# All sixteen tiles through the shared network ahead of the experts, and gated expert rows added to the output in memory

## The chip, the cores and the metric

The kernel is one program on one core of one Trainium2 chip. Its time is the device time of one execution in microseconds (us). The kernel before was timed three times: 1279.81, 1280.91 and 1282.57 us, median 1280.91 us.

## The reference

The layer takes x, 32 batches of 64 rows of 512 floats (2048 tokens), and a context of 1601 rows for each batch. It is three residual blocks, each on the layer norm of its input:

```
x = x + xattn(layernorm(x), ctx)      # similarity to the context, softmax, four features @ W_qv
x = x + attn(layernorm(x))            # 16 heads of 32, causal, 64 rows a batch
x = x + ffn(layernorm(x))
# ffn, h = layernorm(x) of 2048 tokens:
probs = softmax(h @ w_router.T)                     # 8 experts
weight, expert = top_k(probs, 2); weight /= sum(weight)
inter = square(relu(h_of_expert @ w1[e].T))         # 512 -> 512
y     = inter @ w2[e].T                             # 512 -> 512
moe   = sum over both choices of weight * y
shared = square(relu(h @ ws1.T)) @ ws2.T            # 512 -> 1024 -> 512
out   = shared + moe
```

The change is in the third block alone. Every token gets three terms added to its row of x: the shared network, and two gated expert rows.

## The kernel before

The tokens are 16 tiles of 128 rows (T = 16), held in X in on-chip memory. Stage a (the context attention) runs to about 555 us, stage b (the 16-head attention) to about 838 us, and the third block takes the rest. All engines run programs written out by hand: each has its own order of instructions, and they meet at semaphores only. There is no planner. SP issues nearly all DMAs, in one queue; POOL issues the indirect ones.

The third block has these parts.

- **Router.** VectorE (DVE) normalises each tile, TensorE (PE) transposes it (the transposed tiles are h2T), the router's logits are taken, and DVE works out the two experts of each token, their weights (`wt0`, `wt1`, L1672 and L1673) and the slot of each choice (`slot_i`). Slots are rows of `moe_in`, in groups of 128 rows with one expert each: GT = 39 groups, since each expert's last group is padded. `scattered_norm` makes the normed rows of a tile and POOL sends them out with two indirect DMAs (L753), 32 in all.
- **Shared network ahead of the experts.** Tiles 0 to 11 (TA = 12) go in six pairs. PE's `shared(p)` (L2306) does the first layer of pair p in four groups (`shared_group`, at L2064) and then the second layer of both tiles of pair p-1 (`shared_second`, at L2054). Each product is made in three passes, of a high and a low part of every operand, both of type fp32r. ScalarE (ACT) takes the relu and the high part, DVE squares and takes the low part (`shared_rest`), and `residual_c` adds the result to X, counted by `x3_ready`. The transposed tiles 12 to 15 (`h2T_late`) are stored to `h2T_away` by SP (L538), since they stand where the weights of expert 1 go.
- **Weights.** SP loads the high parts of all experts' weights with `load_w1` (L528) and `load_w2` (L532). The last of them, `load_w1(0, 1)` (L601), waits until the first layer of the last pair is done (`sh_done`), since its place holds that pair's data; PE waits for it at L2386, before the first expert group.
- **Experts.** For each group g, SP loads the low parts of the weights where the expert changes (L573) and the 128 rows of the group (L595, four DMAs). DVE transposes the rows (L1642); PE makes the first layer of g and the second layer of g-1 (L2345, L2348, L2351); DVE copies the result from PSUM to one of two buffers `yg` (L1781, counted by `y_ready`); SP stores it to `moe_out` (L625). PE needs the copy of group g-1 before it writes its bank again (L2375).
- **End.** Tiles 12 to 15 go through the shared network after the experts, in float32 and one pass: PE at L2404 and L2412, 32 products each, with weights loaded again. At the same time POOL gathers the two expert rows of each of 16 tiles by indirect DMA (L764), DVE multiplies by the weights and adds them to X (`mix`, L1806 and L1807), and SP stores each tile (L645). X of tiles 0 to 7 was stored to `x_away` and is loaded back.

## Time and profile before

| | us |
|---|---|
| timed runs | 1279.81, 1280.91, 1282.57 |
| the profiled execution's own time | 1278.48 |
| its span, first to last instruction | 1276.8 |
| PE busy | 1251.5 (98%), 7654 matmuls |
| DVE busy | 763.6 (60%) |
| ACT busy | 364.6 (29%) |
| POOL busy | 173.8 (14%) |
| TensorE clock granted, mean | 0.999 |

The span runs from the first to the last instruction of any engine; 1.7 us of the execution lie around it. "Busy" is time in which an engine had an instruction under way. The matmuls' ends are modelled, so a busy PE is not PE at its peak. A DMA's "landing" is the time from its issue to its completion.

### The profile page before, as it was taken

How to read it: one execution, taken by the hardware profiler on the slowest of the kernel's cores; microseconds unless marked ns; L12 is line 12 of the kernel's file. 1: busy time of each engine (PE TensorE's matmuls, PEld its weight loads, DVE VectorE, ACT ScalarE, POOL GpSimd, SP SyncE). 2: the span in 40 equal slices, each digit the busy share in tenths (PEclk: the TensorE clock that was granted, in tenths of full speed). 3: DMA queues.
4: the chain of work that ended last, by engine and by line, in shares of the span. 5: the costliest groups of instructions: out<-in, count | busy, mean ns of one | idle time of the engine just before them, and what ended most of it. 6: DMA issues, size and time to landing. Idle time of an engine off the chain costs nothing.

```text
span 1276.8 us, 21920 instructions
## 1 busy us (share of the span) xinstructions
PE 1251.5 (98%) x7654; PEld 844.2 (66%) x7655; DVE 763.6 (60%) x1409; ACT 364.6 (29%) x593; POOL 173.8 (14%) x159
## 2 busy tenths in 40 slices
PE   5999999999999999999999999999999999999998
PEld 3344444444444444467888888899998888888843
DVE  4456555655454444478988877857543555555556
ACT  2322211212121211244555454542222233332300
POOL 1000000000000000003222223601430000000055
PEclk9999999999999999999999999999999999999999
DMA  9999999999999999833788778731749545554587
GB/s 353 411 418 416 415 415 419 419 419 418 419 419 416 392 396 390 316 134 123 253 285 276 256 266 305 281 132 59 275 170 333 169 155 188 186 185 158 170 324 247
DMA packets 103763, 375.95 MB, mean 294 GB/s; under 512 B 10656, under 2 KB 33184, under 8 KB 88992
## 3 DMA queue, kind: packets, MB, share of 16 engines
q1 hardware_dynamic: 98592, 358.52, 73.6%
q0 software_dynamic: 5120, 16.78, 3.7%
q8 instruction: 28, 0.46, 0.1%
q14 instruction: 23, 0.19, 0.0%
HBM read 368.45 MB, written 69.73 MB: 343 GB/s over the span
## 4 chain that ended last, share of the span: by engine, by line
PE 86%; DMA 7%; DVE 3%; issue 1%; ACT 1%; SPq 1%; POOL 0%; ACTq 0%; DVEq 0%; POOLq 0%
PE ps L1992 14%; PE ps L1880 13%; PE ps L2064 9%; PE ps L2054 9%; PE ps L2345 6%; PE ps L2348 6%; PE ps L2351 6%; DMA parts_low<-split 5%; PE ps L1955 4%; PE ps L1838 3%; PE ps L2412 2%; PE ps L2404 2%; PE ps L1970 2%; DMA arena<-ctx_n 2%; PE ps L1930 1%
## 5 line engine op out<-in xcount | busy, mean ns | idle before, releaser
L1992 PE MATMUL ps<-arena 128*64 128x512 f32 (+1 forms) x832 | 193.1, 596 | 0.0
L1880 PE MATMUL ps<-arena 128*64 128x512 f32 (+1 forms) x1024 | 177.6, 503 | 1.9 <-DVE arena L1138 1.2
L2064 PE MATMUL ps<-split 128*128 128x256 f32 x1344 | 170.6, 285 | 2.6 <-DVE split L1337 2.3
L2064 PEld LDWEIGHTS ps<-split 128*128 128x128 f32 x1344 | 163.7, 191 | 7.2 <-issue 4.7
L1880 PEld LDWEIGHTS ps<-arena 128*64 128x64 f32 x1024 | 65.0, 137 | 122.0 <-issue 119.4
L1992 PEld LDWEIGHTS ps<-arena 128*64 128x64 f32 (+1 forms) x832 | 58.4, 137 | 113.2 <-issue 112.6
L1234 DVE SCALAR_TENSOR_TENSOR arena<-arena,hbar 128x512 f32<-128x512 f32 x128 | 90.5, 749 | 67.9 <-PE ps L1955 66.3
L772 ACT ACTIVATE arena<-ps 128x512 f32<-128x512 f32 (+1 forms) x93 | 52.2, 581 | 241.9 <-PE ps L1955 180.2
L2054 PE MATMUL ps<-split 128*128 128x512 f32 x384 | 96.6, 400 | 1.1 <-DVE arena L1405 1.1
L1208 DVE TENSOR_TENSOR F<-arena,ps 128x512 f32<-128x512 f32 x16 | 11.0, 688 | 135.9 <-ACT split L817 135.9
L678 POOL TENSOR_TENSOR arena<-arena,row_b 128x512 f32 (+1 forms) x16 | 20.2, 1268 | 475.5 <-DVE arena L1108 448.1
L2054 PEld LDWEIGHTS ps<-split 128*128 128x128 f32 x384 | 69.7, 188 | 17.6 <-issue 2.0
L764 POOL DMA_INDIRECT arena<-moe_out,slot_i x32 | 34.0, 1063 | 271.4 <-DMA moe_out<-arena 262.0
L1955 PE MATMUL ps<-arena 128*64 128x512 f32 x256 | 66.0, 594 | 0.3 <-DVE arena L1234 0.3
L2054 PE MATMUL ps<-split_ws,split 128*128 128x512 f32 x264 | 61.1, 390 | 0.0
L817 ACT ACTIVATE split<-ps 128x256 fp32r<-128x256 f32 x32 | 10.5, 381 | 163.9 <-PE ps L1860 163.9
L2054 PEld LDWEIGHTS ps<-split_ws,split 128*128 128x128 f32 x264 | 49.2, 188 | 10.0
L772 ACT ACTIVATE arena<-arena 32x512 f32<-32x512 f32 x64 | 40.3, 630 | 34.0 <-DVE arena L1352 30.8
L1055 ACT ACTIVATE row_a<-ps 128x512 f32<-128x512 f32 x39 | 23.3, 598 | 82.1 <-PE ps L2351 82.1
L2345 PE MATMUL ps<-w_high,xT_p 128*128 x156 | 45.8, 415 | 0.2 <-issue 0.2
L753 POOL DMA_INDIRECT moe_in<-arena,idx x32 | 33.1, 1035 | 89.1 <-DVE idx L1736 81.7
L1838 PE MATMUL ps<-ident,arena 128*128 128x128 f32 x256 | 37.2, 276 | 8.0 <-DVE arena L1108 6.7
(229 smaller groups left out, 2007.5 us busy)
## 6 DMA issues: line engine op xcount, KB each, us to landing
arena<-ctx_t SPq DMA_DIRECT2D x122, 800.5 KB, 17.0
high<-parts_low SPq DMA_DIRECT2D x78, 1024.0 KB
arena<-ctx_n SPq DMA_DIRECT2D x96, 768.0 KB, 13.5
arena<-ctx_n SPq DMA_DIRECT2D x32, 1024.0 KB, 14.8
parts_high<-split SPq DMA_DIRECT2D x16, 1024.0 KB, 8.7
parts_low<-split SPq DMA_DIRECT2D x16, 1024.0 KB, 10.5
moe_in<-zero SPq DMA_DIRECT2D x3, 3328.0 KB, 17.5
moe_out<-arena SPq DMA_DIRECT2D x39, 256.0 KB, 2.1
```

Of the source, the lines that this page charges most:

```text
L764: nc.gpsimd.indirect_dma_start(y01[k][i], None, moe_out, bass.IndirectOffsetOnAxis(ap=slot_i[k][:, t:t + 1], axis=0)).then_inc(y01_in[i % ...
L772: return nc.scalar.activation(o, i, ACT.Copy)
L1234: v.scalar_tensor_tensor(Wc[:, h, :], w_qv_sb[:, 3 * KD + k, :], hbar[:, i, k, h:h + 1], w_qv_sb[:, k, :], ALU.mult, ALU.add).then_inc(wc_ ...
L1838: last = nc.tensor.transpose(dst[:, P * k:P * (k + 1)], src[:, P * k:P * (k + 1)], ident[:, :])
L1880: last = mm(bank(n)[S * h:S * (h + 1), 0:w], qT[:, k, S * h:S * (h + 1)], ctxT[h][:, k, at_j:at_j + w], start=(k == 0), stop=(k == KD - 1))
L1955: last = mm(bank(5)[r, :], F1[i][:, k, r], Wc[:, h, :], start=False, stop=(k == KD - 1))
L1992: last = mm(bank(7)[S * h:S * (h + 1), :], ET[0:w, c, S * h:S * (h + 1)], ctxN[h][0:w, c, :], start=(c == 0), stop=(c == JC - 1))
L2054: last = mm(dst, lhs[a][:, k, :], rhs[b][:, k, :], start=(k + i == 0), stop=(k == n - 1 and i == 2))
L2064: last = mm(dst[:, 2 * P * m:2 * P * (m + 1)], w[a][:, k, c], tokens[b][:, k, :], start=(k + i == 0), stop=(k == KD - 1 and i == 2))
L2345: mm(dst, parts[0][:, k, :], high_w(k), start=(k == 0), stop=False)
L2348: mm(dst, parts[1][:, k, :], high_w(k), start=False, stop=False)
L2351: last = mm(dst, parts[0][:, k, :], low_w(k), start=False, stop=(k == KD - 1))
```

## The change

- `TA` becomes T: all 16 tiles go through the shared network ahead of the experts, in eight pairs. ACT's and DVE's programs have pairs 5 and 6 written out after their loops, without a scatter; PE's loop runs two rounds more. The float32 shared network after the experts goes, with `h2T_away`, the second loads of ws1 and ws2, `x_away` and `moe_out`.
- `out` has 128 rows more than the result, for padded slots; the host drops them. SP stores X with the shared network's part straight to `out` (`store_rows`, five DMAs in all with one that zeroes the extra rows).
- A new table `slot_info` in device memory holds for each of the 39 x 128 slots the token's row and its weight, 8 bytes a slot. SP fills it for empty slots (row 2048 + partition, weight 0); POOL writes the entries of the tokens with 32 indirect DMAs, two a tile; SP waits for all of them and loads the table into `of_slot` with one DMA, ahead of `load_w1(0, 1)` in its queue. DVE turns the rows into integers (`token_i`).
- DVE's copy of each group's result becomes a product by the slot's weight, from `of_slot`.
- POOL adds each group's 128 rows to `out` by one indirect DMA with accumulate; it waits for the DMA of the group before, since two groups may hold the same token. The gathers, `mix`, and the stores at the end go.
- `load_w1(1, 2)` moves behind the low weights of group 0 and waits for the low part of tile 15; `load_low2(g + 1)` waits for PE's `y_done` in place of `y_ready`.

```diff
 TY = (TX + T) // 2
-TA = 3 * T // 4
+TA = T
 TH = T // 2
-TL = T - TR
 S16 = B * S // P
...
     moe_in = nc.dram_tensor("moe_in", [GT * P, D], F32).ap()
-    moe_out = nc.dram_tensor("moe_out", [GT * P, D], F32).ap()
-    x_away = nc.dram_tensor("x_away", [T * P, D], F32).ap()
-    h2T_away = nc.dram_tensor("h2T_away", [P, KD, (T - TR) * P], F32).ap()
+    slot_info = nc.dram_tensor("slot_info", [GT * P, 2], F32).ap()
     parts_high, parts_low = ([nc.dram_tensor(f"{n}{i}", [E * P, KD * D], F32).ap() for i in range(2)]
                              for n in ("parts_high", "parts_low"))

...
+        no_token = sb("no_token", [P, 2])
         cdot, smax, nsmax, smx, erow, rs = (small[:, i:i + 1] for i in range(6))
         bmax, nbmax, bsum, brec = (per_batch[:, i, :] for i in range(4))

         slot_i = [sb(f"slot_i{k}", [P, T], I32) for k in range(2)]
         eg_i = sb("eg_i", [P, GT], I32)
...
             for q in range(1, ZEROED):
                 zero_slots(q)
+            sp.wait_ge(pool_filled, NOTOKEN)
+            info_v = slot_info.rearrange("(g p) c -> p g c", p=P)
+            sp.dma_start(info_v, no_token[:, :].unsqueeze(1).to_broadcast([P, GT, 2])).then_inc(info_filled, 16)
...

             load_w1(5, E)
-            for t in range(TR, T):
-                sp.wait_ge(r_h2T_ready, t + 1)
-                sp.dma_start(h2T_away[:, :, P * (t - TR):P * (t - TR + 1)], h2T_late[t - TR]).then_inc(h2T_moved, 16)
-            sp.wait_ge(h2T_moved, 16 * TL)
-            sp.wait_ge(lg_done, T)
-            load_w1(1, 2)
-
-            away = x_away.rearrange("(t p) d -> p t d", p=P)
+
...
             read_group(0)
             load_low1(0)
-            sp.wait_ge(x3_out, 32)
+            sp.wait_ge(x3_out, 48)
             load_w2(ARENA + KD * D, 7, 8)
+            sp.wait_ge(lg_done, T)
+            sp.wait_ge(h2lo_ready, T)
+            load_w1(1, 2)
+            sp.wait_ge(x3_ready, TR)
+            store_rows(slice(TH, TR))
             for i in range(2):
                 sp.wait_ge(scat[i], 32 * (T // 2))

...

             load_slots(0)
+            sp.wait_ge(info_out, 16 * 2 * T)
+            sp.dma_start(of_slot[:, :, :], info_v).then_inc(info_in, 16)
...
+            sp.wait_ge(x3_ready, T)
+            store_rows(slice(TR, T))

...
                     sp.wait_ge(xgT_ready, g + 2)
                     load_slots(g + 3)
-                if g > 0:
-                    sp.wait_ge(y_ready, g)
-                    sp.dma_start(moe_out[P * (g - 1):P * g, :], yg[(g - 1) % 2]).then_inc(y_out[(g - 1) % 2], 16)
                 if g + 1 < GT:
+                    if g > 0:
+                        sp.wait_ge(y_done, g)
                     load_low2(g + 1)
-                if g in LATE_WS1:
-                    k = LATE_WS1.index(g)
-                    sp.wait_ge(y_done, S16 * (k // 2 + 1))
-                    sp.dma_start(ws1_l[:, k:k + 1, :], ws1t.rearrange("(k p) n -> p k n", p=P)[:, k:k + 1, :]
-                                 ).then_inc(ws_in, 16)
-                if g == GT - 2:
-                    sp.wait_ge(in_done, GT)
-                    sp.dma_start(h2T_l, h2T_away).then_inc(h2T_moved, 16)
-            sp.wait_ge(y_ready, GT)
-            sp.dma_start(moe_out[P * (GT - 1):P * GT, :], yg[(GT - 1) % 2]).then_inc(y_out[(GT - 1) % 2], 16)
-            sp.dma_start(X[:, 0:TH, :], away[:, 0:TH, :]).then_inc(x3_back, 16)
-            sp.dma_start(ws2_l, ws2t.rearrange("(k p) n -> p k n", p=P)).then_inc(ws_in, 16)
-
-            def store_out(t):
-                sp.wait_ge(mix_ready, MIX.index(t) + 1)
-                if t >= TR:
-                    sp.wait_ge(x3_ready, t + 1)
-                sp.dma_start(out_v[:, t:t + 1, :], X[:, t:t + 1, :]).then_inc(out_sem, 16)
-
-            for t in (*range(TH, TR), 0, 1, 2, TR, 3, 4, TR + 1, 5, 6, 7, TR + 2, TR + 3):
-                store_out(t)
-            sp.wait_ge(out_sem, 16 * T)
+            sp.wait_ge(x3_out, 16 * 5)


         @block.gpsimd
...
                         ).then_inc(scat[i], 16)

-            pool.wait_ge(y_out[0], 16 * (GT // 2 + 1))
-            pool.wait_ge(y_out[1], 16 * (GT // 2))
-            for i, t in enumerate(MIX):
-                if i >= 4:
-                    pool.wait_ge(y01_in[i % 4], 32 * (i // 4))
-                    pool.sem_inc(hold, 1)
+            pool.wait_ge(info_ready, 2)
+            pool.wait_ge(pool_filled, IOTA)
+            pool.wait_ge(info_filled, 16)
+            for t in range(T):
                 for k in range(2):
                     nc.gpsimd.indirect_dma_start(
-                        y01[k][i], None, moe_out, bass.IndirectOffsetOnAxis(ap=slot_i[k][:, t:t + 1], axis=0)
-                    ).then_inc(y01_in[i % 4], 16)
+                        slot_info, bass.IndirectOffsetOnAxis(ap=slot_i[k][:, t:t + 1], axis=0), info[k][:, t, :], None
+                    ).then_inc(info_out, 16)
+
+            pool.wait_ge(token_ready, 1)
+            pool.wait_ge(x3_out, 16 * 5)
+            for g in range(GT):
+                pool.wait_ge(y_ready, g + 1)
+                if g > 0:
+                    pool.wait_ge(y_out[(g - 1) % 2], 16 * ((g - 1) // 2 + 1))
+                nc.gpsimd.indirect_dma_start(
+                    out, bass.IndirectOffsetOnAxis(ap=token_i[:, g:g + 1], axis=0), yg[g % 2], None,
+                    compute_op=ALU.add).then_inc(y_out[g % 2], 16)
+            pool.wait_ge(y_out[(GT - 1) % 2], 16 * ((GT - 1) // 2 + 1))
+            pool.wait_ge(y_out[GT % 2], 16 * (GT // 2))


...
             dve.wait_ge(lg_read, 2)

-            def shared(p, scatter):
+            def shared(p, scatter=None):

                 shared_start(p)
-                scattered_norm(scatter)
+                if scatter is not None:
+                    scattered_norm(scatter)
                 shared_residuals(p)
-                scattered_norm(scatter + 1)
+                if scatter is not None:
+                    scattered_norm(scatter + 1)
                 shared_rest(p)

...
             step(v.tensor_tensor(vs, v0, v1, ALU.add))
             step(v.reciprocal(vs, vs))
-            step(v.tensor_tensor(wt0[:, :], v0, vs, ALU.mult))
-            step(v.tensor_tensor(wt1[:, :], v1, vs, ALU.mult))
+            v.tensor_tensor(info[0][:, :, 1], v0, vs, ALU.mult).then_inc(info_ready, 1)
+            v.tensor_tensor(info[1][:, :, 1], v1, vs, ALU.mult).then_inc(info_ready, 1)
...
                 shared(p, scatter=2 * p - 2)
             shared(4, scatter=6)
+            for p in range(5, TA // 2 - 1):
+                shared(p)
...
                     if not (isinstance(stores, int) and stores == 0):
                         dve.wait_ge(y_out[i], 16 * stores)
-                    v.tensor_copy(yg[i], bank(3)).then_inc(y_ready, 1)
+                    gate = of_slot[:, bass.ds(g - 1, 1), 1:2].rearrange("p o c -> p (o c)")
+                    v.tensor_scalar(yg[i], bank(3), gate, None, ALU.mult).then_inc(y_ready, 1)
...
             for i in range(2):
                 residual_c(TA - 2 + i, i)
+            dve.wait_ge(info_in, 16)
+            v.tensor_copy(token_i[:, :], of_slot[:, :, 0]).then_inc(token_ready, 1)
             for g in range(1, 4):
...
             experts(GT - 1, True, True, False, out=out_of(GT - 1))
             experts(GT, False, True, False, out=out_of(GT))
-
-
-            def mix(i):
-                t = MIX[i]
...
-                dve.wait_ge(mix_ready, MIX.index(TR + u) + 1)
-                v.tensor_tensor(x_tile(TR + u), x_tile(TR + u), last_bank[u], ALU.add).then_inc(x3_ready, 1)
-
-            last_square(0)
-            last_square(1)
-            for m, i, n in ((2, 0, 2), (3, 2, 1), (4, 3, 1), (5, 4, 2), (6, 6, 1), (7, 7, 1)):
...
             experts(GT - 1)
             experts(GT, now=False)
-            pe.wait_ge(ws_in, 32 + 16 * KD)
-            pe.wait_ge(h2T_moved, 16 * (TL + 1))
-            pe.wait_ge(x3_ready, TA)
-            for m in range(KF):
...
-            pe.wait_ge(ws_in, 48 + 16 * KD)
-            for u in range(TL):
-                for k in range(KF):
-                    if u == 0:
-                        pe.wait_ge(lsh_ready, k + 1)
-                    last = mm(last_bank[u], shT_l[:, k, P * u:P * (u + 1)], ws2_l[:, k, :],
-                              start=(k == 0), stop=(k == KF - 1))
-                last.then_inc(shared_done, 1)


...
     nc = bacc.Bacc("TRN2", target_bir_lowering=False, num_devices=1, dynamic_dma_scratch_size=4096)
     aps = [nc.dram_tensor(n, a.shape, mybir.dt.from_np(a.dtype), kind="ExternalInput").ap() for n, a in ins.items()]
-    out = nc.dram_tensor(_OUT, (B * S, D), F32, kind="ExternalOutput").ap()
```

## Rows read from the trace of the kernel before

**Rows 1.** The chain that ended last, its final pieces: start us, us, what.
```profile
1217.68 0.93 PE ps L2351 x4
1218.61 27.47 PE ps L2404 x64
1246.08 27.48 PE ps L2412 x64
1273.58 0.69 DVE arena L1818
```

**Rows 2.** Timeline of PE, last shared pairs and first expert group: start, us, instruction.
```profile
906.77 11.68 PE L2064 MATMUL ps<-split 128*128 128x256 f32 x96
918.28 11.07 PE L2054 MATMUL ps<-split_ws,split 128*128 128x512 f32 x48
929.19 11.68 PE L2064 MATMUL ps<-split 128*128 128x256 f32 x96
...
951.61 11.68 PE L2064 MATMUL ps<-split 128*128 128x256 f32 x96
963.12 11.07 PE L2054 MATMUL ps<-split_ws,split 128*128 128x512 f32 x48
974.43 1.20 PE L2345 MATMUL ps<-w_high,xT_p 128*128 x4 [0.23 <-issue]
```

**Rows 3.** Timeline of DVE: result copies of four expert groups, and a PSUM product.
```profile
1100.94 0.69 DVE L1781 COPY arena<-ps 128x512 f32<-128x512 f32 x1 [0.61 <-PE ps L2351]
1106.88 0.69 DVE L1781 COPY arena<-ps 128x512 f32<-128x512 f32 x1 [0.62 <-PE ps L2351]
1214.06 0.69 DVE L1781 COPY arena<-ps 128x512 f32<-128x512 f32 x1 [1.46 <-PE ps L2351]
1218.65 0.69 DVE L1781 COPY arena<-ps 128x512 f32<-128x512 f32 x1 [2.83 <-PE ps L2351]
1222.08 0.69 DVE L1812 TENSOR_SCALAR arena<-ps 128x512 f32<-128x512 f32 x1 [2.74 <-PE ps L2404]
```

**Rows 4.** Line L753 (the 32 indirect stores): its instructions, and issue to landing.
```profile
L753 POOL DMA_INDIRECT moe_in<-arena,idx x32: 958/974/1242, 888.1 to 958.8; - x32
DMA to landing us min/median/max: 2.7/3.0/8.3
```

**Rows 5.** Line L764 (the 32 gathers), the same two rows.
```profile
L764 POOL DMA_INDIRECT arena<-moe_out,slot_i x32: 942/1018/1333, 1221.9 to 1264.4; - x32
DMA to landing us min/median/max: 3.6/6.0/6.7
```

**Rows 6.** Stretches: engines' busy us, clock, DMA share, GB/s.
```profile
core 0: us, PE busy (x) PEld busy (x) DVE busy (x) ACT busy (x) POOL busy (x), PEclk, DMA share, GB/s
1050.00:1100.00 50.00, 50.00 (x238) 41.35 (x237) 28.53 (x43) 15.87 (x26) 0.00 (x0) 1.00 0.54 179
```

**Rows 7.** Timeline of SP's DMA issues before the first expert group.
```profile
965.95 1.75 SPq L595 DMA_DIRECT2D arena<-moe_in  x4
967.75 1.21 SPq L528 DMA_DIRECT2D w_high<-parts_high  x1
969.00 0.95 SPq L532 DMA_DIRECT2D high<-parts_high  x2
970.82 1.82 SPq L595 DMA_DIRECT2D arena<-moe_in  x4
972.68 0.45 SPq L532 DMA_DIRECT2D high<-parts_high  x1
```

**Rows 8.** DMAs issued in 967 to 974 us: count, KB each, median us to landing.
```profile
high<-parts_high SPq DMA_DIRECT2D x2, 2048.0 KB, 12.6
w_high<-parts_high SPq DMA_DIRECT2D x1, 1024.0 KB, 5.6
```

**Rows 9.** DMA in 1110.8 to 1114 us, a group's rows loaded: packets, queue's share.
```profile
DMA packets 577, 0.26 MB, mean 82 GB/s; under 512 B 65, under 2 KB 577, under 8 KB 577
q1 hardware_dynamic: 577, 0.26, 29.3%
```

**Rows 10.** Waits of SP's queue in 840 to 1000 us: total, times, longest.
```profile
SPq L593 <- DMA arena<-moe_in: 9.3, 1, 9.3
SPq L588 <- DMA moe_in<-arena,idx: 8.0, 1, 8.0
```

**Rows 11.** Timeline of SP's issues around the end of stage b.
```profile
802.32 8.51 SPq L500 DMA_DIRECT2D moe_in<-zero  x2
837.24 0.36 SPq L528 DMA_DIRECT2D w_high<-parts_high  x1
```

**Rows 12.** Timeline of PE: second layer of the first expert group.
```profile
988.54 1.17 PE L2345 MATMUL ps<-w_high,xT_p 128*128 x4
...
991.37 1.07 PE L2345 MATMUL ps<-high 128*128 x4
```

86 lines of the change are left out of this document (27 added, 59 removed).

## The prediction, made before the changed kernel ran

> **What bounds the kernel now.** I read the page's shares first, then the chain of waits, then the timelines of PE, DVE, SP and POOL around the changed places, and last the landings of the DMAs. The page gives PE as busy for 98% of the span, and the chain runs through PE to its end: the last second-layer product of the last expert group ends at 1218.61, two blocks of 64 float32 products follow, 27.47 and 27.48 us, and one DVE addition ends the arithmetic at 1274.3 of 1276.8 [rows 1]. So the time is a sum of PE's own durations. The pieces around the change are regular: one shared pair takes 22.42 us on PE, 906.77 to 929.19 to 951.61 [rows 2], and an expert group 5.94 us, 1100.94 to 1106.88 [rows 3]. No wait of note stands in either. The DMA engines are half used in the expert stage, a share of 0.54 [rows 6].
>
> **The part that goes.** Everything after 1218.61 goes: both float32 blocks, the gathers, the mixing, and the last stores. 1276.8 - 1218.61 = 58.2 us of the span. Gathers, mixing and the reload of X ran beside the float32 products and are worth nothing by themselves; with the products they go in full.
>
> **The part that comes instead, on PE.** Two more pairs, 2 x 22.42 = 44.8 us [rows 2]. The range of this term is small: in the pairs before, DVE also made and scattered two tiles' rows and PE still had no gap, and the new pairs have less on DVE. ACT and DVE run the same program a pair. DVE's, ACT's and PE's own durations in them I take as unchanged.
>
> **The new end.** After PE's last product DVE multiplies by the weight in place of a copy. A copy from PSUM took 0.69 us and so did a tensor-scalar product from PSUM [rows 3], so this edit is free in every group, and 0.04 + 0.69 us at the end. Then POOL issues the last accumulating DMA and waits for its landing. No row shows an accumulating DMA. The nearest is the plain indirect store of the same 128 rows of 2 KB, 3.0 us from issue to landing, 2.7 at the least and 8.3 at the most [rows 4]; the gathers, issued while the engines were full, took 3.6 to 6.7, median 6.0 [rows 5]. Below 2.7 it can't be, since it does all that the store does. I take 4.0: the store's 3.0 and one more for reading the old rows, at a time with no other transfer. With 0.3 for the last wait the end costs 0.7 + 4.0 + 0.3 = 5.0 us; by the bounds 3.7 to 9.3.
>
> **The accumulating DMAs before the last.** There are 39, each waits for the landing of the one before, and nothing else holds POOL, whose issue takes 1.0 us [rows 4]. They are hidden as long as one takes less than a group's 5.94 us from issue to landing. The cover is two `yg` buffers: DVE's product waits for the landing of two groups before, PE's next second layer waits for that product, so a landing that is late once is absorbed and a mean above 5.9 us is not. From 4.0 there are 1.9 us of room, and I cost this at nothing; by the upper row of the loaded gathers it costs (second rival). In bytes it takes the place of the store to `moe_out`, and adds a read of 256 KB a group; 179 GB/s on average at a share of 0.54 [rows 6] leaves room. The first one also waits for the last store of X, 1 MB queued behind the low weights of group 1; PE's chain waits for no accumulate until the third group's result, two groups later, so that is hidden.
>
> The Trainium skill (Collectives: The Full Stack, The bandwidth ceiling: the fold count and why AG ≠ RS ≠ AR) says that an add in the DMA path is slow by its second source read, with twice the read traffic, and not by the add. By that rule the transfer part of the 256 KB would double, an estimate of some 0.7 us, and the landing would be 3.7 in place of my 4.0, 0.3 us less in the sum.
>
> **The slot table.** POOL's 32 small indirect stores follow its last row store, 958.8 + 1.3, since the scatters stand in the same pairs as before [rows 4]. The gathers' starts are (1264.4 - 1221.9) / 31 = 1.37 us apart [rows 5]; 32 of them end at 960.1 + 43.9 = 1004, and with 3.0 us from the last issue all have landed at about 1006. SP is by then past `load_slots(0)` and its wait for the scatters, which in the kernel before still cost it 8.0 us [rows 10]. The last pair's first layer, 963.1 before, ends at 963.1 + 44.8 = 1007.9 [rows 2]. So the load of the table goes out at about 1006 and `load_w1(0, 1)` directly behind it at 1008.3, in the same queue. PE wants that weight at 974.19 + 44.84 = 1019.0 (974.43 less the 0.23 us of issue [rows 2]). Before, it was issued at 967.75 [rows 7] and landed 5.6 us later at 973.4 [rows 8], 0.8 us ahead of PE: this margin is thin, but SP now issues it 10.7 us ahead in place of 6.4.
>
> What eats this is the table's load itself. Slots of a group lie along the partitions, so the 39 x 128 entries of 8 bytes are 4992 separate pieces, 312 for each of 16 engines. The smallest pieces in the trace are the 512-byte ones of a group's rows: 577 packets in a share of 0.293 of 3.2 us and 16 engines, 26 ns each [rows 9]. By that the table takes 312 x 0.026 = 8.1 us, about 1007.5 to 1015.6; the weight's 1 MB needs some 3 us of the queue and its latency, and lands at 1019 to 1021. I take a stall of 1.0 us on PE. It can be 0 (smaller pieces may be quicker than 512 bytes) or, at four times 26 ns, (312 x 0.104 = 32.4 us, 24.3 more) about 25 us; nothing in the trace bounds it closer. The other weights behind it have more room: `load_w2(4, 6)`, issued at 972.68 and 12.6 us under way, was there by 985.3, and PE asks at 991.4 [rows 7, 8, 12].
>
> The Trainium skill (DMA: Bandwidth & Descriptors, Specifications) says that below 512 bytes a transfer is done as read-modify-write. That speaks against the table: if a piece then costs twice the 26 ns, the stall is 1.0 + 8.1 = 9.1 us, which is the first rival; no row has pieces this small.
>
> **Edits at nothing.** SP fills the table once with the same 4992 pieces after the zeroing of the slots, issued at 802, and its next load is only at 837.24 [rows 11]; that weight is used 150 us later. The stores of tiles 12 to 15 to `h2T_away` go; they lay beside PE. `load_w1(1, 2)` moves some 125 us later, to about 987, when the low part of tile 15 is done, still 32 us ahead of PE. `load_low2` waits for `y_done`, a copy earlier than before. Two weight products lose their step waits, four iotas and memsets come on POOL where it idles.
>
> **The sum**, against the profiled execution: 1276.8 - 58.2 + 44.8 + 5.0 + 1.0 = 1269.4 us of span, with 1.7 us around it 1271.1. The median of the timed runs stood 2.4 us above the profiled execution (1280.91 against 1278.48), so the forecast is 1273.5 us, 7.4 less than before. Its own range, from the bounds of the end and a stall of up to 3 us, is 1271 to 1280.
>
> **Rivals.**
> 1. *The table's load stands in front of the weight.* Every nanosecond over 26 a piece costs 0.31 us of PE. At 52 ns the time is 1281.6, at 58 the gain is gone, at 104 it is 1298. For: 8-byte pieces, the same queue, and the 0.8 us margin of before. Against: 512-byte pieces also carry their bytes, so a piece of 8 may be no slower. Chance 0.17, over 1278 to 1298.
> 2. *The accumulating DMAs become the chain* (the other side). The place is POOL's wait for the group before; it decides from 5.9 us on. At 6.7, the slowest gather, the 38 intervals cost 38 x (6.8 - 5.94) = 33 us and the time is 1306; at the slowest store, 8.3, 38 x 2.46 = 93 us and 1367. PE would then wait at L2375 in every group. For: one at a time, a read and a write in memory at both ends, full engines when an expert's weights load. Against: the median plain store at 3.0, and only some of the groups load weights. Chance 0.21.
> 3. *Something small eats it*: a landing of 8 us at the end (+4), or PE losing a little in each group to slower loads. 1276 to 1282. Chance 0.06.
>
> The forecast has 0.56. **Range and chances.** Two medians of this kernel can be told apart from 0.2%, 2.6 us on. The forecast's 0.56 is all faster but for 0.01. Rival 1 gives 0.02 faster, 0.05 same and 0.10 slower; rival 2 is slower, 0.21; rival 3 splits 0.03, 0.02, 0.01. Faster 0.60, same 0.08, slower 0.32. The range goes from 1270 to 1306, where the slower half of rival 2 is left out.
>
> **What would show it.** Right: PE without a gap from the first added pair to about 1263; no float32 block; a product at L1781's place every 5.94 us; the indirect DMAs landing in about 4 us; the end some 5 us after PE's last product. Rival 1 shows as one gap of PE ahead of the first expert group, with SP's weight landing late. Rival 2 shows as a gap of PE in each group, DVE waiting for an accumulating DMA, and a group's period equal to its landing. The forecast is wrong if either gap is over 5 us in sum, or a shared pair takes other than 22.4 us.

## The result, and the profile after

The changed kernel takes 1294.22 us in the median of four runs (1286.60 to 1298.28) against 1280.36 of the kernel before on the same chip: a ratio of 1.0107, with a 95% interval of 1.0083 to 1.0132. It is slower by 1.1%, where the forecast was 1273.5 us, 0.6% faster. The profiled execution is the quickest of the four, 1286.6 us with a span of 1284.9, so the trace explains 15.5 of the 20.7 us between forecast and median (1284.9 against the forecast span of 1269.4); the other executions have no trace. Here and below, a ratio is that of a kernel's time to the kernel before on the same chip, and the bracket behind it its 95% interval.

The page of the changed kernel: busy time by engine, then the groups of the chain, then POOL's accumulating DMA and the product by the weight.

```profile
PE 1244.3 (97%) x7814; PEld 861.6 (67%) x7815; DVE 743.3 (58%) x1382; ACT 376.1 (29%) x613; POOL 233.0 (18%) x202
...
DMA out<-arena,token_i 16%; PE ps L1950 14%; PE ps L2022 14%; PE ps L2012 13%; PE ps L1838 13%; PE ps L1913 4%; PE ps L1796 2%; PE ps L1928 2%; DMA arena<-ctx_n 2%; PE ps L1888 1%; PE ps L2041 1%; PE ps L1895 1%; PE ps L1892 1%; PE ps L1902 1%; PE ps L1900 1%
...
L742 POOL DMA_INDIRECT out<-arena,token_i x39 | 60.6, 1554 | 217.3 <-DMA out<-arena,token_i 151.4
...
L1768 DVE TENSOR_SCALAR arena<-ps,of_slot 128x512 f32<-128x512 f32 x39 | 29.3, 751 | 71.6 <-DMA out<-arena,token_i 60.2
```

PE is busy 7.2 us less than before and the span is 8.1 us longer. The chain, which before ran through PE to its last product [rows 1], now has 16% of accumulating DMAs in it. PE's timeline (start, us, instruction) shows how far the forecast holds:

```profile
904.00 11.68 PE L2022 MATMUL ps<-split 128*128 128x256 f32 x96
...
926.41 11.68 PE L2022 MATMUL ps<-split 128*128 128x256 f32 x96
...
948.84 11.68 PE L2022 MATMUL ps<-split 128*128 128x256 f32 x96
...
971.25 11.68 PE L2022 MATMUL ps<-split 128*128 128x256 f32 x96
...
1005.19 11.07 PE L2012 MATMUL ps<-split_ws,split 128*128 128x512 f32 x48
1016.09 1.07 PE L2303 MATMUL ps<-w_high,xT_p 128*128 x4
```

A pair is still 22.42 us, as in [rows 2], no gap stands ahead of the first expert group, and this execution came to that stretch 2.8 us earlier than the one before did. SP's queue shows why the first expert's weight was in time:

```profile
1005.27 0.38 SPq L583 DMA_DIRECT2D of_slot<-slot_info  x1
1005.70 2.66 SPq L512 DMA_DIRECT2D w_high<-parts_high  x1
```

```profile
of_slot<-slot_info SPq DMA_DIRECT2D x1, 39.0 KB, 4.7
```

The second fence is the list of DMAs (KB, us to landing): the table of 4992 pieces landed 4.7 us after its issue. What went wrong comes behind it, in POOL's adds (duration, first and last start, who is waited for, landings), where [rows 4] had 958 ns and 3.0 us:

```profile
L742 POOL DMA_INDIRECT out<-arena,token_i x39: 1550/1550/1611, 1037.8 to 1278.7; - x39
its engine sat idle before it (us, times) until:
  DMA out<-arena,token_i: 151.4, 32
  DVE arena L1768: 65.9, 7
who waited for it (us, times):
  POOL out L742: 151.4, 32
  DVE arena L1768: 60.2, 26
...
DMA to landing us min/median/max: 4.4/5.0/8.3
```

39 starts from 1037.8 to 1278.7 are 38 intervals of 6.34 us, against 5.94 for a group before [rows 3]. 32 of the 38 waited for the landing of the add before, and 26 times DVE then waited for its buffer. PE in turn waits for DVE's product (us in total, times, longest), which is a part of what it loses in the expert groups:

```profile
PE ps L2303 <- DVE arena L1768: 7.1, 4, 2.9
```

The last pieces of the chain (start, us, what) show two turns:

```profile
1268.01 4.40 DMA out<-arena,token_i
1272.40 0.02 issue
...
1272.45 0.71 issue
1273.16 4.81 DMA out<-arena,token_i
1277.97 0.02 issue
...
1278.01 0.50 issue
...
1278.53 0.19 issue
1278.72 1.55 POOL out L742
```

A turn is the landing and 0.75 us more until POOL starts the next. So the cover ends at a landing of 5.2 us (5.94 - 0.75) and not at 5.9; the median of 5.0 is just inside, the late ones up to 8.3 are not. PE's last product starts at 1270.67 and ends at about 1271.7, and the span ends 13.2 us later: three adds are still to land then, the one issued at 1268.01 and the two behind it.

### The profile page after: what moved, and what is told of

Read it like the earlier page. It is cut to its first block, busy times and chain, and to the rows that moved or that the text cites. A ratio compares the mean times of both kernels' runs of the same rounds, so it can differ in the third digit from the quotient of the medians.

```text
span 1284.9 us, 22350 instructions
## 1 busy us (share of the span) xinstructions
PE 1244.3 (97%) x7814; PEld 861.6 (67%) x7815; DVE 743.3 (58%) x1382; ACT 376.1 (29%) x613; POOL 233.0 (18%) x202
## 4 chain that ended last, share of the span: by engine, by line
PE 76%; DMA 17%; issue 3%; DVE 2%; ACT 1%; SPq 1%; POOL 0%; POOLq 0%; DVEq 0%; ACTq 0%
DMA out<-arena,token_i 16%; PE ps L1950 14%; PE ps L2022 14%; PE ps L2012 13%; PE ps L1838 13%; PE ps L1913 4%; PE ps L1796 2%; PE ps L1928 2%; DMA arena<-ctx_n 2%; PE ps L1888 1%; PE ps L2041 1%; PE ps L1895 1%; PE ps L1892 1%; PE ps L1902 1%; PE ps L1900 1%
## 5 line engine op out<-in xcount | busy, mean ns | idle before, releaser
L2022 PE MATMUL ps<-split 128*128 128x256 f32 x1536 | 194.0, 285 | 1.4 <-DVE split L1319 1.2
L2022 PEld LDWEIGHTS ps<-split 128*128 128x128 f32 x1536 | 187.0, 191 | 6.1 <-issue 4.9
L642 POOL TENSOR_TENSOR arena<-arena,row_b 128x512 f32 (+1 forms) x16 | 20.3, 1270 | 474.3 <-DVE arena L1090 446.4
L742 POOL DMA_INDIRECT out<-arena,token_i x39 | 60.6, 1554 | 217.3 <-DMA out<-arena,token_i 151.4
L2012 PE MATMUL ps<-split_ws,split 128*128 128x512 f32 x360 | 83.5, 390 | 0.1
L2012 PEld LDWEIGHTS ps<-split 128*128 128x128 f32 x384 | 69.7, 188 | 17.8 <-issue 2.0
L2012 PEld LDWEIGHTS ps<-split_ws,split 128*128 128x128 f32 x360 | 67.1, 188 | 14.1 <-DVE split L1564 0.5
L1768 DVE TENSOR_SCALAR arena<-ps,of_slot 128x512 f32<-128x512 f32 x39 | 29.3, 751 | 71.6 <-DMA out<-arena,token_i 60.2
L2303 PE MATMUL ps<-high 128*128 x156 | 43.2, 399 | 8.4 <-DVE arena L1768 7.1
```

Of the source, the lines that this page charges most:

```text
L742: nc.gpsimd.indirect_dma_start(out, bass.IndirectOffsetOnAxis(ap=token_i[:, g:g + 1], axis=0), yg[g % 2], None, compute_op=ALU.add).then_i ...
L1768: v.tensor_scalar(yg[i], bank(3), gate, None, ALU.mult).then_inc(y_ready, 1)
L2012: last = mm(dst, lhs[a][:, k, :], rhs[b][:, k, :], start=(k + i == 0), stop=(k == n - 1 and i == 2))
L2022: last = mm(dst[:, 2 * P * m:2 * P * (m + 1)], w[a][:, k, c], tokens[b][:, k, :], start=(k + i == 0), stop=(k == KD - 1 and i == 2))
L2303: mm(dst, parts[0][:, k, :], high_w(k), start=(k == 0), stop=False)
```

## The experiments

Theory A: the adds, one at a time, are the loss. Its parts are an add that lands in 5.0 us instead of 3.0, the 0.75 us behind it, and the weight loads that lift the mean; with two buffers PE can't run ahead. Rival B: any indirect DMA from POOL in every group costs this, whatever it does. Rival C: part of the loss is elsewhere, in the product by the weight, the slot table or the earlier stores of X. The first four kernels ran on one chip, beside the kernel before (1280.47 us, nine runs).

**e1_plain**: a store in place of the add, so that the output holds the last writer's rows.

```diff
-                    out, ..., yg[g % 2], None,
-                    compute_op=ALU.add).then_inc(y_out[g % 2], 16)
+                    out, ..., yg[g % 2], None).then_inc(y_out[g % 2], 16)
```

> The 39 indirect DMAs store their rows instead of adding them (the sum with X and the second expert row is lost); still one at a time. Theory A (the chain of adds is the bound, by the landing of an accumulating DMA): landing falls from a median of 5.0 us to 3.0 to 3.5, below a group's 5.9 us, PE's gaps in the expert stage go, 1268 to 1275 us. Rival B (an indirect DMA from POOL in every group costs this whatever it does, by its issue or its traffic beside the weight loads): unchanged, 1286 to 1298 us.

Measured 1268.27 us, ratio 0.9903 (0.9868 to 0.9939).

```profile
L742 POOL DMA_INDIRECT out<-arena,token_i x39: 958/958/967, 1038.5 to 1262.5; - x39
its engine sat idle before it (us, times) until:
  DVE arena L1767: 210.9, 37
  DMA out<-arena,token_i: 11.6, 2
```

The wait for the DMA before is still there and costs 11.6 us of POOL in place of 151.4; 37 times POOL waits for data. The median landing is 2.7 us, the slowest 6.0. Rival B falls: it is the accumulate, and not the indirect store or its wait.

**e2_noadd**: no adds and no waits for them; the experts' part is missing from the output.

```diff
-            for g in range(GT):
-                pool.wait_ge(y_ready, g + 1)
-                ...indirect_dma_start(out, ..., compute_op=ALU.add)
+            pool.wait_ge(y_ready, GT)
```

> The adds of the expert rows are left out with their waits; all else of the change stays. This prices everything but the adds. Theory A: the expert stage takes 244 us on PE as before the change, and the kernel ends about 2 us after its last product: 1262 to 1267 us. Rival C (part of the loss is elsewhere: the gate on DVE, the slot table, the earlier stores of X): 1272 us or more.

Measured 1266.46 us, ratio 0.9895 (0.9865 to 0.9925). This is PE's own time for the rest of the change, with 1.7 us behind its last product, and rival C falls on this chip.

**e4_four**: four buffers for the results in place of two, the adds still one at a time.

```diff
-        y_out = [sem(f"y_out{i}") for i in range(2)]
+        y_out = [sem(f"y_out{i}") for i in range(4)]
+        yg += [X[:, TH + i, :] for i in range(2)]
```

> Four result buffers in place of two (two of them in tiles of X that have been stored), the adds still one at a time. Theory A: PE's gaps of 11 us vanish, but the chain of 39 adds has the same sum and the wait moves to the end: 1284 to 1298 us, not told from the changed kernel. Rival D (the adds fit on average and only their jitter hurts, two buffers being too few to absorb it): 1270 to 1277 us.

Measured 1291.86 us, ratio 1.0090 (1.0062 to 1.0118). POOL's first and last start in its trace are 1037.0 and 1287.3, 6.59 us apart on the mean. The total is as theory A has it, but PE's gaps didn't vanish: its expert groups still take 254.0 us (1015.3 to 1269.3), and 24.6 us stand behind its last product in place of 13.2. DVE waited 17 times for a buffer, 26 before. More buffers put off a chain that is too slow but don't shorten it, and four fill up too.

**e5_nolow**: the low halves of the weights are loaded once, so that the DMA engines have less to do beside the adds (all groups use expert 0's low halves).

```diff
-                cond=group[g] != group[g - 1] if g > 0 else None
+                cond=group[g] > 2 * E if g > 0 else None
...
-                lo = places[0] + odd * (places[1] - places[0])
+                lo = places[0]
```

> The low parts of the weights are loaded once, for group 0, and not again where the expert changes (all groups use those; some 14 MB of loads fall away from the expert stage). Adds one at a time. Theory A with the loads as what lifts the mean: every add lands in 4.4 to 5.2 us, period 5.2 to 5.9, just under a group's 5.92: 1268 to 1276 us. Theory A without them (the add alone is too slow): landings of 8 us stay, 1286 to 1298 us.

Measured 1270.37 us, ratio 0.9921 (0.9893 to 0.9949).

```profile
L742 POOL DMA_INDIRECT out<-arena,token_i x39: 1550/1550/1611, 1040.7 to 1265.7; - x39
its engine sat idle before it (us, times) until:
  DVE arena L1768: 184.0, 35
  DMA out<-arena,token_i: 17.5, 4
```

The adds are all there, each waits for the one before, and they follow DVE at 5.92 us: their slowest landing fell from 8.3 to 5.8 us. So an add by itself fits into a group; what breaks it is the add beside the weight loads. (The low parts are the only weights that SP loads while most of the groups run, so this kernel also frees the queue for all other loads, which the run can't part.)

Two rows of the output can only meet in two adds if these belong to different experts, since a token's two choices differ. So the wait is needed only where the expert changes. The next three were made to find the version that keeps the gain; they ran on another chip (before there 1277.75).

**e3_two**: odd groups add into a second table, so each add waits for the one two before (half of the experts' rows are then missing from the output).

```diff
-                if g > 0:
-                    pool.wait_ge(y_out[(g - 1) % 2], 16 * ((g - 1) // 2 + 1))
+                if g > 1:
+                    pool.wait_ge(y_out[g % 2], 16 * (g // 2))
...
-                    out, ...
+                    (out, other)[g % 2], ...
```

> Groups of odd number are added to a second table in device memory, which nothing merges with the first (half of the expert rows are missing from the result); each add waits only for the one two groups before. The adds' number, form and bytes stay, so the traffic stays and the chain is cut in two. Theory A (one at a time is what binds): two adds in flight, PE's gaps go, the end 5 to 6 us after PE's last product, 1268 to 1275 us. Rival E (the adds' traffic beside the weight loads is too much for the DMA engines, one at a time or two): 1284 us or more.

Measured 1303.62 us, ratio 1.0189 (1.0163 to 1.0215).

**e6_dyn2**: the wait for the add before only where the expert changes, for the groups from 3 to 31.

```diff
+                last, here = here, pool.value_load(eg_i[0:1, g:g + 1], ...)
...
+                if g > 1:
+                    pool.wait_ge(y_out[(g - 2) % 2], 16 * ((g - 2) // 2 + 1))
+                if 0 < g < 3 or g >= 32:
                     pool.wait_ge(y_out[(g - 1) % 2], 16 * ((g - 1) // 2 + 1))
+                elif g > 0:
+                    pool.wait_ge(y_out[(g - 1) % 2], 16 * ((g - 1) // 2) + 16 * (here != last))
```

> Two buffers as in the changed kernel, but an add waits for the one just before it only where the expert changes (and before group 3 and from group 32 on); otherwise for the one two groups before. Two groups of one expert hold different tokens, so the result is whole. Theory A: most adds overlap; the full landing of 7 to 8 us is still waited for at the seven changes of expert, where the weight loads lie: 1270 to 1277 us. If two in flight are no faster than one (rival E): 1284 us or more.

Measured 1303.52 us, ratio 1.0200 (1.0171 to 1.0228).

**e7_dyn4**: the same with the four buffers of e4_four.

> As the run before with four buffers in place of two (before group 5 and from group 32 on one at a time). Theory A: the waits at the changes of expert no longer reach PE, 1268 to 1273 us, level with the run that stores instead of adding. If four buffers bring nothing over two here, 1270 to 1277 us as that run.

Measured 1302.46 us, ratio 1.0189 (1.0162 to 1.0216).

All three missed, 26 to 30 us above their ranges. Their expert stage did what was expected: in e3_two POOL waits 12.9 us for DMAs, and PE is busy 149.66 of the 150 us from 1050 to 1200, where it is 144.80 in the changed kernel. But the first add starts at 1071.3, where the changed kernel's stood at 1037.8. The loss lies ahead of the experts, in a stretch that the first four kernels had run through without a gap. Theory G: it belongs to the chip or the execution. Rival H: it belongs to the altered code. Four kernels on a third chip (before 1280.44) tell them apart, three of them copies: **c1_after** is the changed kernel, **c2_noadd** a copy of e2_noadd, **c3_dyn2** of e6_dyn2.

> The changed kernel again, unaltered. Open is why three variants (e3_two, e6_dyn2, e7_dyn4) whose expert stage ran with no gap on TensorE took 1302 to 1304 us: all of their loss lies between 967 and 1005 us, where TensorE, ScalarE and VectorE stood with gaps of up to 2.4 us between single instructions while GpSimd issued its 32 eight-byte stores to the table of tokens and gates. Theory G (the gap belongs to the chip or the execution, not to those variants' code): on a chip where the variant with the relaxed wait shows it, this one shows it in some of its executions too, about 30 us later than the 1286.6 us seen, so 1300 to 1318; on a chip without it 1286 to 1295. Rival H (the gap belongs to the altered code): 1286 to 1298 here whatever the variant does.

Measured 1321.83 us (1316.90 to 1326.40), ratio 1.0320 (1.0266 to 1.0374): 4 us above theory G's range.

> The variant without the accumulating DMAs and their waits, which took 1266.5 us and had no such gap. G: with the gap about 1295, without 1266. H: 1266, since this code had none.

Measured 1297.49 us, ratio 1.0129 (1.0086 to 1.0172), 31.0 above its twin.

> The variant that waits for the add before only where the expert changes, which took 1303.5 us with the gap. G: if this chip has none, 1303.5 less about 33 us, so 1268 to 1274, below both kernels; if it has it, 1303 again and the two above have it too. H: 1302 to 1305 again on any chip.

Measured 1305.94 us, ratio 1.0197 (1.0154 to 1.0240).

**e8_half**: the changed kernel with the table's small stores for the even tiles alone; half of the experts' rows are not added.

```diff
-            for t in range(T):
+            for t in range(0, T, 2):
```

> The changed kernel with half of the table's small stores (even tiles alone; half of the rows then are not added). If the small stores are what keeps the engines from their instructions, the gap, where it is shown, is about half as long: 15 to 18 us instead of 33, between 967 and 983 us; where the changed kernel shows no gap, this one shows none, and takes 1268 to 1280 since fewer rows are added. If the gap is of something else in that stretch, it stays at about 33 us.

Measured 1301.98 us, ratio 1.0172 (1.0119 to 1.0226); with half a gap on top of 1268 to 1280 it should have stood at 1283 to 1298, so the time misses by 4 us. What it had wrong is the adds: an empty slot's row is added too (to the extra rows of `out`, with weight 0), so the 39 adds keep their size and their chain, 6.33 us apart here. The reading on the gap rests on the trace. The stretches of c1_after, the changed kernel with the gap (us busy and instructions by engine, clock, DMA share, GB/s):

```profile
core 0: us, PE busy (x) PEld busy (x) DVE busy (x) ACT busy (x) POOL busy (x), PEclk, DMA share, GB/s
...
957.00:967.00 10.00, 10.00 (x65) 9.08 (x65) 2.01 (x3) 1.20 (x2) 7.56 (x9) 1.00 0.69 265
967.00:977.00 10.00, 4.68 (x17) 3.09 (x15) 1.29 (x2) 1.15 (x2) 7.56 (x9) 0.84 0.02 1
977.00:987.00 10.00, 4.15 (x7) 1.94 (x7) 0.00 (x0) 0.00 (x0) 7.56 (x9) 0.50 0.02 1
987.00:997.00 10.00, 2.51 (x5) 1.15 (x4) 0.00 (x0) 0.00 (x0) 5.52 (x6) 0.50 0.02 1
997.00:1007.00 10.00, 7.21 (x27) 6.38 (x28) 2.38 (x4) 1.58 (x3) 3.83 (x4) 0.50 0.01 0
1007.00:1017.00 10.00, 10.00 (x76) 9.74 (x76) 4.88 (x8) 4.27 (x8) 0.00 (x0) 0.96 0.00 1
```

The same kernel, in the execution that was profiled first:

```profile
967.00:977.00 10.00, 10.00 (x68) 9.26 (x67) 3.97 (x7) 3.50 (x7) 7.87 (x8) 1.00 0.02 1
977.00:987.00 10.00, 10.00 (x69) 9.28 (x68) 3.30 (x5) 2.34 (x4) 7.56 (x9) 1.00 0.24 15
```

And e8_half:

```profile
967.00:977.00 10.00, 6.87 (x27) 4.72 (x26) 1.30 (x2) 1.15 (x2) 7.56 (x9) 0.94 0.02 1
977.00:987.00 10.00, 6.36 (x13) 3.83 (x13) 0.69 (x1) 0.00 (x0) 3.79 (x4) 0.50 0.01 1
987.00:997.00 10.00, 10.00 (x76) 10.00 (x76) 5.99 (x9) 4.70 (x8) 0.00 (x0) 0.88 0.00 1
```

While POOL issues its stores of eight-byte pieces with no other transfer under way, from 977 to 997 PE gets through 5 to 7 matmuls in 10 us, VectorE and ScalarE through none, and POOL itself runs at its usual pace. PE's granted clock is 1.00 up to 967, 0.84 in the stretch in which PE was busy 4.68 us of 10, 0.50 (the 1.2 GHz level) in the three behind it, and 0.96 once PE runs whole again. Two lines of c1_after's timeline (start, us, instruction, and in brackets the idle time before it and its releaser):

```profile
991.68 0.59 PE L2012 MATMUL ps<-split_ws,split 128*128 128x512 f32 x1 [2.22 <-issue]
...
998.73 0.69 DVE L1570 TENSOR_TENSOR arena<-arena,ps 128x512 f32<-128x512 f32 x1 [28.26 <-remote]
```

PE's gaps are named "issue": they wait for no semaphore that the trace shows. VectorE's wait is for a semaphore for which the trace names no engine ("remote"), and it isn't PE's slowness handed on. This addition needs the first 24 of a pair's 48 second-layer products. In c4_dyn2, the run without a gap below, it starts 5.7 us after PE starts those products; here PE starts them at 961.73 and has done 31 by 968.95, and VectorE adds at 998.73, 37 us on. PE was whole, though, while the first eight small stores went out (958.83 to 967.83), with other transfers still under way up to about 964. With 16 stores in place of 32 the engines are back at 987 instead of about 1005, and the first add starts at 1054.5 instead of 1070.6: 16 us less for 16 stores less. Theory G holds: by its times the same code has the gap in every execution on one chip and in none on another (c2_noadd, 1296 to 1300 us, and e2_noadd, 1266 to 1269), and e3_two, e6_dyn2 and e7_dyn4 show it on a second chip.

Is it the size of the pieces, or that the stores stand alone? The next four ran on a fourth chip (before 1279.04), with **c4_dyn2**, again a copy of e6_dyn2, as their control.

> The variant with the relaxed wait once more, as it is, to see whether this chip has the gap between 967 and 1005 us. With the gap 1303 to 1306, without it 1268 to 1274. It is the base of e9_wide and e10_mixed.

Measured 1275.00 us (1271.53 to 1279.19, ten runs), ratio 0.9966 (0.9952 to 0.9979), 1 us above its range. No gap on this chip, and the relaxed wait makes the change 0.3% faster than the kernel before. As this chip has no gap, none of the three runs beside it can tell what makes one.

**e9_wide**: rows of 512 bytes in the table, the first eight bytes of which count.

```diff
-    slot_info = nc.dram_tensor("slot_info", [GT * P, 2], F32).ap()
+    slot_info = nc.dram_tensor("slot_info", [GT * P, 128], F32).ap()
...
-                        slot_info, ..., info[k][:, t, :], None
+                        slot_info, ..., info_w[k][:, 2 * t:2 * t + 128], None
```

> The same with rows of 512 bytes in the table of tokens and gates, so that each small store writes 512 bytes where it wrote 8 (the first 8 count). If what holds the engines back is the size of the pieces (eight bytes), the gap goes and the time is 1268 to 1276. If it is the run of 32 indirect DMAs with nothing between them, whatever they write, the gap stays at 30 to 35 us and the time at 1300 to 1308.

Measured 1273.87 us, ratio 0.9962 (0.9949 to 0.9976). It tells nothing on the gap, since the control had none.

**e10_mixed**: each tile's two small stores right behind its two of rows.

```diff
-            with pool.Fori(0, T // 2) as n:
+            for n in range(T // 2):
...
+                    for k in range(2):
+                        ...indirect_dma_start(slot_info, ..., info[k][:, t, :], None)
```

> The same with each tile's two small stores issued right behind its two stores of rows, so that the 32 are spread over 886 to 970 us among 256 KB stores instead of running alone in 957 to 1005 us. If they hold the engines back only as a run by themselves, no gap is left and the time is 1268 to 1274, below both kernels. If each small store costs TensorE about 1 us wherever it stands (16 fewer took 16 us off), the gap is only spread, TensorE's pairs grow from 22.4 to about 29 us in that stretch, and the time is 1298 to 1308.

Measured 1292.99 us, ratio 1.0118 (1.0094 to 1.0141): a miss for both expectations. Its waits from 880 to 1020 us (total, times, longest):

```profile
ACT row_a L973 <- DVE split L1572: 33.7, 6, 20.2
...
DVE arena L1554 <- DMA moe_in<-arena,idx: 28.8, 7, 7.5
...
PE ps L2030 <- ACT row_a L973: 15.8, 1, 15.8
```

The small stores held back those of the rows in POOL's queue; DVE waited for their landing to free its buffer (28.8 us, where c4_dyn2 has 5.0), and DVE's next work for the shared network is behind that wait. One gap of 16 us on PE followed, by a plain wait and not by the effect of before. Whether spread small stores would spare PE on a chip with the gap stays open.

**e11_chain**: the same spread stores, with the adds one at a time.

> The changed kernel, its adds one at a time as written, with only the small stores spread in the same way. It parts the two losses: without the gap and with the chain of adds it should take 1284 to 1292 on any chip, 14 to 20 us above e10_mixed and 30 to 35 below the 1321.8 us of the changed kernel with the gap. If the spread stores still cost their 1 us each, 1316 to 1326.

Measured 1309.32 us, ratio 1.0235 (1.0210 to 1.0261). It misses by the same gap, 16.2 us of PE here, and the 30 to 35 us below c1_after became 12.5; its distance to e10_mixed, 16.3 us, is the price of the chain on one chip with all else equal. c1_after less c3_dyn2 gives 15.9.

**e12_gaps**: 20 of the small stores in POOL's waits for its next rows, 12 at the end. It and the next ran on the first chip of the experiments (before 1279.75).

```diff
+                    here = {7: 6, 9: 4, 11: 6, 13: 4, 15: 12}.get(2 * n + i, 0)
+                    for m in range(small, small + here):
+                        ...indirect_dma_start(slot_info, ..., info[m % 2][:, m // 2, :], None)
```

> The variant with the relaxed wait, with 20 of the 32 small stores put into the times when GpSimd waits for its next rows (6 behind tile 7, 4 behind tile 9, 6 behind 11, 4 behind 13), so that 12 are left to run by themselves at the end (e10_mixed had put them behind every tile, and TensorE stood 16 us at 911 to 927 us for the rows' landings). The first 20 delay no rows here. On a chip without the gap it takes 1271 to 1277, as the variant itself (1275.0). On a chip with it: if small stores hold the engines back only where they run alone, 12 of them leave a gap of 12 to 13 us and the time is 1283 to 1288; if each costs 1 us wherever it stands, 1300 to 1308.

Measured 1277.75 us (1274.36 to 1287.56), ratio 1.0000 (0.9978 to 1.0023). No gap at the last 12, on a chip whose first four kernels had none either. Eight of the twelve executions took 1274 to 1279 us and four 1285 to 1288, the profiled one among these. In it DVE again waited for rows (16.4 us in all), and PE with it (6.9 us): the spread stores did delay rows, which I had excluded.

**c5_wide** is a copy of e9_wide.

> The variant with 512-byte rows in the table once more, unaltered, since the chip of its first run had no gap in any kernel. If e12_gaps shows this chip to have the gap: size of the pieces decides, then none here and 1271 to 1278; the run of 32 stores decides, then 30 to 35 us of gap and 1300 to 1308. On a chip without the gap 1271 to 1278 whatever decides.

Measured 1274.44 us (1272.69 to 1276.61, nine runs), ratio 0.9960 (0.9948 to 0.9973). POOL's adds in it:

```profile
L752 POOL DMA_INDIRECT out<-arena,token_i x39: 1550/1550/1611, 1040.4 to 1267.9; - x39
...
  DMA out<-arena,token_i: 57.8, 13
```

The intervals are (1267.9 - 1040.4) / 38 = 5.99 us: a group's period, and not that of a landing. This chip has no gap either, so the size of the pieces stays open.

**e13_sizes**: e9_wide with 12 eight-byte stores into an unused table in front of its 32.

```diff
+            for t in range(12):
+                ...indirect_dma_start(dump, ..., info[0][:, t, :], None)
```

> The variant with 512-byte rows in the table, with 12 stores of eight bytes into a table that nobody reads put in front of its 32. So one profile holds both sizes, one behind the other, on one chip: GpSimd issues the small ones at about 960 to 975 us and the wide ones at 975 to 1020. The table comes 16 us later and SP's loads of the first expert's weights with it, so TensorE has to wait some 10 to 18 us at the first group whatever holds. On a chip with the gap: if the size of the pieces decides, TensorE, VectorE and ScalarE stand with short gaps while the 12 are issued and run whole while the 32 are; if the run of stores decides, the gaps go on to 1020 us (44 us of them). On a chip without the gap neither part shows any, and the time is 1284 to 1294; then the size stays open.

Measured 1285.98 us, ratio 1.0046 (1.0029 to 1.0063), on a fifth chip (before 1280.00), where neither part showed a gap. The 32 eight-byte stores in a row never ran there. What it shows is the table's margin: the table's load goes out at 1019.97 in place of 1005.27, and PE stands 10.9 us at the first group.

```profile
1017.00:1027.00 10.00, 1.17 (x6) 0.63 (x4) 4.66 (x7) 3.49 (x6) 1.38 (x2) 0.74 0.60 113
```

## Why the prediction was wrong

**The step that failed is "The accumulating DMAs before the last": "From 4.0 there are 1.9 us of room, and I cost this at nothing."** The runs showed a chain that bounds the kernel, for three reasons. The landing was 5.0 us in the median and not 4.0. The 0.75 us between a landing and the next issue had no term at all, though the second rival's working added 0.1 for it. And the mean decides, not the median: the plain stores of before reached 8.3 us [rows 4] and so did the adds, and e5_nolow ties this to the weight loads (5.8 at most without the low parts). The mean turn was 6.34 us against a group's 5.94. The rule was in the prediction ("a mean above 5.9 us is not" absorbed) and was then fed with a quiet value of the landing.

The sum against the span of the profiled execution, forecast 1269.4 and measured 1284.9:

| | forecast | measured | difference |
|---|---|---|---|
| first expert group starts | 1020.2 (974.4 + 44.8 + 1.0) | 1016.1 | -4.1 |
| expert groups on PE | 244.2 (974.4 to 1218.6) | 255.6 (1016.1 to 1271.7) | +11.4 |
| from PE's last product to the end | 5.0 | 13.2 | +8.2 |

- *The part that goes, the part that comes*: right. 58.2 us of float32 work gone, 2 x 22.42 us added, no gap in the new pairs on this chip. The first group came 4.1 us early, 2.8 of them because this execution ran ahead before the change began, and 1.0 because the stall wasn't there.
- *The new end*: the landing at the end was under-sized (4.0 for about 5), but most of the 8.2 us is the queue of adds behind PE. It belongs to the failed step. The bound of 9.3 didn't hold, because it took one add to be left.
- *The slot table*: right in its place and time (load at 1005.27, forecast 1006), too high in price. 4.7 us for 312 pieces an engine is at most 15 ns a piece, against 26 taken, so the stall of 1.0 us wasn't there and rival 1 is refuted here. (Its working has a slip: by its own 0.31 us a nanosecond, the gain of 7.4 us is gone at 50 ns a piece and not at 58, as its 1281.6 us at 52 ns says too.) The Trainium skill (DMA: Bandwidth & Descriptors, Specifications) has transfers below 512 bytes done as read-modify-write; for this load the trace shows no such cost. e13_sizes shows that the margin is real: 16 us later, and PE waits.
- *Rival 2* was the mechanism, at its threshold and not at its price: 6.34 a turn where it worked with 6.8 and up. That the measured time lies within the stated 1270 to 1306 is owed to this rival and not to the forecast. It says "decides from 5.9 us on"; with the 0.75 us it decides at a landing of 5.2. Its chance of 0.21 was too low for a wait whose operation no row had shown, and whose margin was less than the spread of the rows nearest to it.
- The Trainium skill (Collectives: The Full Stack, The bandwidth ceiling: the fold count and why AG ≠ RS ≠ AR) prices the second source read and no more, for adds between cores in a ring. By it I had 3.7 us; the trace has 4.4 at the least, and POOL's issue grew from 958 to 1550 ns, which such a rule can't see. Trace and rule differ, and the measurement decides.

With the wait relaxed (c4_dyn2, c5_wide) the kernel takes 1275.0 and 1274.4 us: the rest of the forecast, 1273.5 with the adds hidden, was right within 1.5 us. That closeness is partly luck. In e9_wide's trace, the same kernel as c5_wide with a span of 1271.1, PE's first group starts 3.4 us earlier than forecast (1016.8), the groups take 246.1 us in place of 244.2 (to 1262.9), and the end 8.2 in place of 5.0; the last seven adds still go one at a time there. The gain of the change went into the chain of adds, 16 us of it, shown by two pairs of runs that differ in that wait alone.

**What no step had** is the second loss, some 31 us on two of five chips of the experiments (c2_noadd less e2_noadd 31.0, c3_dyn2 less c4_dyn2 30.9). It played no part in the profiled execution, nor, at 1294 to 1298 us, in its full size in the three others. Shown is that it stands beside the table's small stores and shrinks with their number (32 against 16, in one pair of runs). The kernel before, which has none of them, keeps its time on both chips (1277.75 and 1280.44). Left open is its mechanism, whether 512-byte pieces or other transfers beside them avoid it, and what differs between the chips, since no variant of the stores but e8_half ran where the gap is. On those two chips each version that ran is slower than the kernel before. On the fourth the relaxed wait makes it 0.3% faster, or 0.4% with the 512-byte rows; on the first it was run only with the 512-byte rows, 0.4% faster, and with the stores moved (e12_gaps), level; on the fifth only e13_sizes ran. No version here is shown to beat the kernel before on all of them, and the one with the 512-byte rows never ran where the gap is.

Open too is why the three untraced executions took 7.4 to 11.7 us more than the profiled one. Kernels with the adds one at a time spread widely (1286 to 1296 in e4_four, 1317 to 1326 in c1_after), and c3_dyn2 beside c1_after by only 1.8 us, which speaks for the landings; but c4_dyn2 spreads by 7.7 us over ten executions without that chain, and no trace shows the difference.

## What to carry to other kernels

A chain of DMAs that wait for each other has the period landing plus reissue, and it must be set against the mean landing beside the heaviest transfers, with the reissue read from a row. If the operation has no row, its price is unknown, and a margin smaller than the spread of the nearest rows isn't cover. Before ordering such operations one by one, ask which of them can touch the same data: here only groups of different experts could, and a wait on those alone gave 16 us back.

The second loss stood on two chips of five and in none of the first four experiments. A comparison on one chip, however often it is repeated, can miss a loss of 31 us.

## What the runs showed of the hardware

- An indirect DMA with accumulate of 128 rows of 2 KB: 1.55 us of POOL and 4.4 us to landing at the least, median 5.0, up to 8.7 with weight loads in the same stage (e11_chain) and 5.8 without (e5_nolow); the plain store 0.96 us of POOL and 2.7 to landing (e1_plain), up to 6.0. From the landing to the start of POOL's next indirect DMA that waits for it, 0.75 us.
- 32 indirect stores of 128 pieces of eight bytes, back to back with nothing else moving: on two chips they kept PE, VectorE and ScalarE from almost all work for some 31 us, about 1 us a store, while POOL ran on; on two others and in the first profile they cost nothing (on the fifth chip only 12 of them ran, at no cost). The 256 KB stores of rows, issued at the same pace in runs of four, did no such thing on any chip.
- Loading 4992 eight-byte pieces into 128 partitions took 4.5 to 5.0 us.
